# The last block of attention crosses into the next stage undivided, with its row of sums

## What is computed

```python
attn = softmax(where(mask, q @ k.T / sqrt(64), min))     # per head, 2048 x 2048
y = attn @ v
x = x + einsum('bqhd,hdo->bqo', y, Wout)                 # out-projection and residual
for j in range(2):
    residual = xf
    ...                                                  # router, top 2 of 6 experts, shared expert
    xf = rmsnorm(residual + combined + share_out) * norm_w[j]
x = x + xf
```

## Time and profile before

| | |
|---|---|
| Runs | 2822.72 us median of 3 (2819.69 to 2826.23) |
| Profiled execution | 2841.7 us, span 2839.9 us |
| Granted TensorE clock, mean | 0.964 |
| Busy | PE 92%, PEld 77%, DVE 69%, ACT 63%, POOL 68% |
| Chain that ended last | PE 23%, DVE 4%, issue 3%, POOL 2%, DMA 2% |

### The profile page before, as it was taken

The page is one execution under the profiler, slowest core; times in us unless marked ns, Lnnn a source line. Parts: engine busy times, 40 slices in busy tenths (PEclk is TensorE's granted clock), DMA queues, the critical chain, the costliest instruction groups (busy, mean ns, idle before and its releaser), DMA issues. The chain is left out here.

```text
span 2839.9 us, 47115 instructions
## 1 busy us (share of the span) xinstructions
PE 2621.3 (92%) x13460; PEld 2183.2 (77%) x13460; DVE 1961.6 (69%) x4391; ACT 1801.4 (63%) x4164; POOL 1933.1 (68%) x1735
## 2 busy tenths in 40 slices
PE   6999999999989999999999999889998998879884
PEld 4787887887768878888888888678887887768773
DVE  7787787787787777787777788345655464754455
ACT  2677777777767777777777777633325663236552
POOL 3698898898878888889889889732352232543234
PEclk8999999999999999999999999999999998889997
DMA  3011111111111110111111001154343441224552
GB/s 72 23 47 40 40 40 48 34 29 42 36 43 37 29 27 18 27 33 26 27 33 24 24 20 24 25 188 135 116 160 125 142 153 59 94 103 151 176 169 81
DMA packets 162956, 193.11 MB, mean 68 GB/s; under 512 B 58114, under 2 KB 126984, under 8 KB 162196
## 3 DMA queue, kind: packets, MB, share of 16 engines
q1 hardware_dynamic: 149396, 156.26, 18.8%
q0 software_dynamic: 12288, 33.57, 3.5%
q10 hardware_dynamic: 1024, 0.26, 0.0%
HBM read 116.02 MB, written 83.16 MB: 70 GB/s over the span
## 5 line engine op out<-in xcount | busy, mean ns | idle before, releaser
L305 POOL TENSOR_TENSOR pl<-pr,ph 128x512 fp32r<-128x512 f32 (+3 forms) x1184 | 1374.0, 1184 | 208.7 <-ACT ph L731 190.9
L728 ACT ACTIVATE pr<-ps 128x512 f32<-128x512 f32 (+3 forms) x1280 | 688.1, 538 | 406.9 <-PE ps L481 173.2
L1003 DVE TENSOR_REDUCE part<-ps 128x1 f32<-128x512 f32 (+3 forms) x1152 | 703.9, 617 | 130.6 <-PE ps L466 115.0
L731 ACT ACTIVATE ph<-ps 128x512 fp32r<-128x512 f32 (+3 forms) x1280 | 686.7, 537 | 0.0
L466 PE MATMUL ps<-k_hi,q_parts 128*128 128x512 f32 (+3 forms) x1280 | 490.1, 384 | 52.5 <-DVE part L1003 46.7
L480 PE MATMUL ps<-q_parts,k_hi 128*128 128x512 f32 (+3 forms) x1280 | 482.8, 377 | 0.3
L481 PE MATMUL ps<-q_row,k_lo 65*128 65x512 f32 (+3 forms) x1280 | 471.8, 369 | 0.0
L466 PEld LDWEIGHTS ps<-k_hi,q_parts 128*128 128x128 f32 x1280 | 243.3, 190 | 140.3 <-DVE part L1003 66.3
L480 PEld LDWEIGHTS ps<-q_parts,k_hi 128*128 128x128 f32 x1280 | 242.1, 189 | 55.2 <-ACT ph L731 7.6
L481 PEld LDWEIGHTS ps<-q_row,k_lo 65*128 65x128 f32 x1280 | 242.6, 190 | 34.2
L1651 PE MATMUL ps<-exp_up,yy 128*128 x888 | 248.4, 416 | 2.2 <-ACT yy L1822 2.1
(11 more groups left out here) (256 smaller groups left out, 4614.4 us busy)
## 6 DMA issues: line engine op xcount, KB each, us to landing
work<-x_slots SPq DMA_DIRECT2D x148, 128.0 KB
e_slots<-work SPq DMA_DIRECT2D x148, 128.0 KB
rec<-recip_rows SPq DMA_DIRECT2D x128, 128.0 KB
y_latent<-y_sums SPq DMA_DIRECT2D x128, 128.0 KB
yg<-y_latent SPq DMA_DIRECT2D x32, 512.0 KB
x_slots<-zero_rows SPq DMA_DIRECT2D x32, 296.0 KB
acc_shared<-accw SPq DMA_DIRECT2D x14, 512.0 KB
accr<-acc_shared SPq DMA_DIRECT2D x12, 512.0 KB
```

Source lines behind the costliest of these rows:

```text
L305: eng.tensor_tensor(pl[:, s % RING, 0:w], pr[:, s % PR_RING, 0:w], f32(ph[:, s % RING, 0:w]), ALU.subtract).then_inc(sem, 1)
L728: act.activation(pr[:, s % PR_RING, 0:w], src, ACT.Exp).then_inc(S["probs"], 1)
L731: act.activation(ph[:, s % RING, 0:w], src, ACT.Exp).then_inc(S["probs_hi"], 1)
L1003: ins = dve.tensor_reduce(dst, src[:, 0:w], AX.X, ALU.max)
```

## The change

For the last block alone (turn 15, second head, query block 3) SP skips `divide`. At the end, `hand_over` sends one row of sums (1 x 512) to a DRAM tensor `last_sums` and stores the block undivided; a wait for the sums is added. VectorE's two late jobs go. In the token stage SP loads `last_sums` as 64 equal rows of 512 into the upper half of a buffer that is free then; VectorE inverts them (`invert_sums`, 64 x 512) in `block_of(4)` and multiplies the 64 rows of y in place (`divide_last`) in `block_of(5)`; ScalarE's `split_y(7, 7)` waits for that.

```diff
+                def hand_over():
+                    last = TURNS - 1
+                    sp.wait_ge(S["y_copied"], 8 * TURNS)
+                    sp.dma_start(last_sums, y[LD:LD + 1, QB - 1, :]).then_inc(S["sums_kept"], DMA)
+                    sp.dma_start(y_dram[last // PAIRS][QB - 1, LD:P, last % PAIRS, :], y[0:LD, QB - 1, :]).then_inc(S[f"stored{QB - 1}"], DMA)
...
                 def turn(p, more, first=False):
                     for half in range(2):
                         for qb in range(QB):
-                            divide(p, half, qb)
+                            if (p, half, qb) != (TURNS - 1, 1, QB - 1):
+                                divide(p, half, qb)
...
-                store(TURNS - 1, 1, QB - 1)
+                hand_over()
                 for qb in range(QB):
                     sp.wait_ge(S[f"stored{qb}"], DMA * 2 * TURNS)
+                sp.wait_ge(S["sums_kept"], DMA)
...
                 turns(dve, turn)
-                late_jobs(invert, INVERT_AFTER)
-                late_jobs(divide, DIVIDE_AFTER)
...
+        last_rows = F["accr"][LD:P, 1].rearrange("p j d -> p (j d)")[:, 0:BLK]
...
+                sp.dma_start(last_rows, last_sums.broadcast_to([LD, BLK])).then_inc(S["sums_in"], DMA)
                 load_x(1)
                 store_x1(0)
...
+                    if (r, pair) == (7, PAIRS - 1):
+                        act.wait_ge(S["last_y"], 1)
...
+                def invert_sums():
+                    dve.wait_ge(S["sums_in"], DMA)
+                    dve.reciprocal(last_rows, last_rows).then_inc(S["inverse"], 1)
+
+                def divide_last():
+                    i = (PAIRS - 1) // 2
+                    dve.wait_ge(S[f"y_in{i % 2}"], DMA * (2 * 7 + i // 2 + 1))
+                    dve.wait_ge(S["inverse"], 1)
+                    rows = y_raw[LD:P, (PAIRS - 1) % 4, :]
+                    dve.tensor_tensor(rows, rows, last_rows, ALU.mult).then_inc(S["last_y"], 1)
...
                     if r + 2 < 8:
                         y_lo_even(r + 2, 4)
+                        if r + 2 == 7:
+                            divide_last()
                         y_lo_even(r + 2, 6)
+                        if r + 2 == 6:
+                            invert_sums()
                         residual(r + 2)
```

More of the change, by code:

```diff
@@ L138, in block_end, with build_attention @@
     return 2 * (qb + 1) * (qb + 2) - 1
-def build_attention(nc, T, w, y_dram, recip_rows, zero_rows, x_slots, m_kept, n_kept):
+def build_attention(nc, T, w, y_dram, last_sums, recip_rows, zero_rows, x_slots, m_kept, n_kept):
     with ExitStack() as ctx:
@@ L183, in build_attention @@
                  "row_in0", "row_in1", "row_in2", "row_in3",
-                 "cleared", "kept", "n_back"]
+                 "cleared", "kept", "n_back", "sums_kept"]
         S = {n: ctx.enter_context(nc.semaphore("a_" + n)) for n in names}
@@ L1147, with build_tokens @@
 LATE = (14, 15)
-def build_tokens(nc, W, F, w, x_v, out_v, y_v, x_slots, e_slots, acc_dram, x1_dram, bias_dram):
+def build_tokens(nc, W, F, w, x_v, out_v, y_v, last_sums, x_slots, e_slots, acc_dram, x1_dram, bias_dram):
     with ExitStack() as ctx:
@@ L1155, in build_tokens @@
                  "router_hi", "router_lo", "w_hi", "w_lo", "made", "bias_made", "share_bias", "own_bias", "bias_sum", "bias_kept", "bias_hi", "bias_lo", "up_table_in",
-                 "y_in0", "y_in1", "x_in0", "x_in1",
+                 "y_in0", "y_in1", "x_in0", "x_in1", "sums_in", "inverse", "last_y",
                  "y_hi", "y_lo_even", "y_lo_odd", "proj", "x1", "x1_stored0", "x1_stored1",
@@ L2511, in norm_at, with build_mixture @@
     return 8 * c + k // 8 if k >= 0 and k % 8 == 0 and k // 8 < QB - 1 else None
-def build_mixture(nc, W, w, y_dram, x_slots, out):
+def build_mixture(nc, W, w, y_dram, last_sums, x_slots, out):
     e_slots = [nc.dram_tensor(f"e_slots{b}", [SLOTS, D], F32).ap() for b in range(B)]
@@ L2561, in build_mixture @@
         y_v = y_dram.rearrange("b q p h n -> (b q) p h n")
-        build_tokens(nc, W, F, w, x_v, out_v, y_v, x_slots, e_slots, acc_dram, x1_dram, bias_dram)
+        build_tokens(nc, W, F, w, x_v, out_v, y_v, last_sums, x_slots, e_slots, acc_dram, x1_dram, bias_dram)
 def build(nc, w, out):
     y_dram = nc.dram_tensor("y_latent", [B, QB, P, PAIRS, BLK], F32).ap()
+    last_sums = nc.dram_tensor("last_sums", [1, BLK], F32).ap()
     recip_rows = nc.dram_tensor("recip_rows", [QB, P, TPB], F32).ap()
@@ L2576, in build @@
             A = dict(T) | attention_tensors(nc, attention, T["nn"])
-            build_attention(nc, A, w, y_dram, recip_rows, zero_rows, x_slots, m_kept, n_kept)
-        build_mixture(nc, T, w, y_dram, x_slots, out)
+            build_attention(nc, A, w, y_dram, last_sums, recip_rows, zero_rows, x_slots, m_kept, n_kept)
+        build_mixture(nc, T, w, y_dram, last_sums, x_slots, out)
 def kernel(L0_attn_x_bld, L0_attn_Wq, L0_attn_Wkv_down, L0_attn_Wk_up, L0_attn_Wv_up, L0_attn_Wout,
```

## The result

The change took 2811.41 us, median of 5 runs (2807.43 to 2814.72), against 2822.72 before (2819.68 to 2826.23). The medians are 11.3 us apart. The text goes by the ratio, which is 0.9965 with a 95% interval from 0.9949 to 0.9982: 9.9 us less, and anything from 5.1 to 14.4 would agree with these runs. The profiled execution has a span of 2813.0 us at a mean granted clock of 0.968; before it was 2839.9 at 0.964.

The account below looks back on a forecast made before the run. TensorE was busy 92% of the span, but the change touches the seam where it stands still. Terms -7.50 + 0.3 + 0 + 0 = -7.2 us took 2822.72 to 2815.5 us, range 2811.5 to 2820.5.

Parts of the forecast that it names:

- The seam: Between attention and token stage: three DMAs, reciprocal, multiplication and their waits go, first load 7.50 us earlier.
- other floor: Rival at the seam: something else ends late or the token stage gives time back, gain say 3 us; chance 0.09.
- The broadcast: Token stage start-up: 64 rows of 2 KB on SP's queue ahead of y(1,0) cost 0.3 us, ends 0 and 2.5.
- the argument by gaps: Token stage start-up: 0.70 us of broadcast work meets 0.75 us of free DMA engine time before y(1,0).
- the rival's 2.0: Token stage start-up: broadcast blocks the queue, y(1,0) waits 2.0 us longer, plus 0.5 of issue; chance 0.14.
- The reciprocal: VectorE, block 4: 1.4 us plus 0.16, hidden in 4.46 us of idle time before the residual; 0 us on the path.
- The slower rival: Block 4: reciprocal takes 21.6 us, delays block 6's residual and makes the total +10.0 us; chance 0.03.
- point of decision: Block 4: the reciprocal costs time only from a length of 4.46 us, VectorE's idle time before the residual.
- The division: VectorE, block 5, between splits of pairs 4 and 6: waits for GpSimd, 0 us on the path, ends 0 and 0.6.
- The clock: TensorE after the seam: clock has fallen by the first products, which start at 1.2 GHz as today; no gain.
- The end of -4.1: Whole kernel: smallest forecast gain, -7.2 + 2.5 + 0.6 us, with both blockings (broadcast and division).
- the blocking's 2.5: Token stage start-up: broadcast holds all queued behind it, 2.0 us plus 0.5 of issue; as a rival, chance 0.14.

Follow-up runs that it names:

- the second trace of before: The kernel before, run once more with no edit beside the repeated change: ratio 1.0004 to the kernel before, seam 11.02 us.
- the threefold reciprocal: The change with the 64x512 reciprocal done three times in a row in block 4: ratio 1.0009 to the kernel before.
- The change, again: The change run once more with no edit, in a second measurement: ratio 0.9973 to the kernel before, which ran at 2844.5 us there.

## Why the prediction was right

**The seam.** 7.50 us foretold, 7.71 measured (11.33 against 3.62; 7.40 against the second trace of before). The store's way to the first load kept its length (3.25 for 3.30). The term was short by 0.2, mostly because the row of sums issues in 0.30 us, not in the 0.49 of the scattered one. The sums landed before the block, and no other floor came up: with the wait gone, the seam went down to 2.07.

**The broadcast.** 0.3 us foretold, nothing seen within a scatter of 1 to 1.6 us. No run tells 0.3 from 0, so the argument by gaps is neither shown nor refuted. Each further broadcast cost 0.7 to 1.1 us, the 0.70 of engine time or somewhat more; the rival's 2.0 was too much.

**The reciprocal.** Right on the path (0 us), wrong in its length: 1.4 us plus 0.16 foretold, 3.35 measured. The step that failed is "the 11 ns difference over 4 elements gives 2.8 ns each": it takes the fixed part of a reciprocal to be that of another operation. From its own two sizes, 3349 - 169 ns over 508 elements, it is 6.3 ns an element and 144 ns fixed (a line through two points, one with 128 partitions, one with 64). The estimate from the Trainium skill (VectorE: DVE Perf Modes, "First, the fixed hardware budget") was 4.3 us; the measurement decides and lies nearer to it than to mine. The slower rival needed 21.6 us. Its point of decision, 4.46 us, is confirmed by the threefold reciprocal, so it was 1.1 us from costing anything: that 0 us came true with a length more than twice the one foretold was partly luck.

**The division.** Foretold 0 us on the path, with the order of events; each came: the multiplication stood until GpSimd was done, GpSimd's pair 5 was held as long as today, pairs 6 and 7 came late with room to spare. The rule of the Trainium skill (SBUF — State Buffer, "Who interferes with whom"), that such a pair blocks each other for a whole instruction, fits this row: 0.68 us of work, 1.69 on the timeline.

**The clock** gave nothing, as foretold: 0.50 when the first products came. At the second projection the two first traces differ: before, TensorE stood idle for 2.46 us and was granted 0.50 from 1876 to 1878; with the change it stood idle for 1.97 us and kept 1.00 from 1868 to 1880. The change, again, fell there too (0.50 from 1872 to 1878 after 2.79 us), so this is scatter.

**The sum.** -7.2 foretold. The first measurement gave -9.9 (-14.4 to -5.1), the second -7.7 (-13.1 to -2.3 by its interval, of 2844.5). The median of 2811.41 us lies 4.1 below the forecast of 2815.5 and 0.1 below the range's lower end of 2811.5; by the ratio it is 2812.8. The traces hold no extra that would bring it there: up to the residual of block 7 the change gains 7.4 us in the mean, the seam's 7.7 within the scatter. The run times, whose intervals are 5 us wide to each side, can't exclude 2 us more behind it. The end of -4.1 in the prediction adds the blocking's 2.5 to a sum that already holds 0.3 for the broadcast; from the seam's 7.50 it would be -4.4. Nothing hung on it.

## What to carry to other kernels

Where every engine waits for one last piece, count the DMA round trips that this piece makes alone, and let the piece cross undone if a later stage can finish it beside other work: here three DMAs in a row, with the waits between them, were worth 7.7 us, and the finishing showed no cost: the reciprocal and the multiplication fitted waits already there. The wait in front of the next instruction is a budget, and for the reciprocal it was exact to 0.01 us; price what you put in it from its own sizes, not from a small case. A small gain is better shown by the steps of the trace than by the total: two executions of one program differed by 23 us in the part that the change doesn't touch.

## What the runs showed of the hardware

A reciprocal in fp32 on VectorE takes 6.3 ns an element of a partition beyond 144 ns fixed, by its two sizes (169 ns for 4 elements, 3.35 us for 512). The larger is five times the 0.68 us of a multiplication of the same 64x512. GpSimd's indirect DMAs beside it were not held up: they ran at 0.96 us each (the first at 1.25), as before. A row of 2 KB from one partition issues in 0.30 us as the first of two stores, but in 0.49 when it follows the block.
